# Two attention layers over 16 graphs: TensorE's items dealt anew over the steps, with new places for loads and statistics

## The chip, the cores and the metric

One core of one Trainium2 chip. The metric is the device time of one launch in microseconds. Before the change it is 2078.54 us, the median of 3 runs (2071.99 to 2079.57).

## The reference

For each of 16 graphs `x` is (512, 384) and `adj` (512, 512), all float32, 12 heads of 32:

```
h = relu(layernorm(x)); q, k, v = h@Wq+bq, h@Wk+bk, h@Wv+bv
s = q k^T / sqrt(32) + beta*adj, masked where adj <= 0;  x = x + softmax(s) v          (layer 0)
h = relu(layernorm(x)); q, k, v = h@Wq^T, h@Wk^T, h@Wv^T+bv
s = q k^T / sqrt(384) + 2*adj, rows that are all zero give 0; x = x + softmax(s) v @ Wo^T + bo  (layer 1)
```

## The kernel before, in words

The 32 graph passes (16 graphs in layer 0, then 16 in layer 1; `g`) are cut into 3 chunks `c` of 4 heads, and each chunk into 4 steps `t`, one for each 128 query rows: 12 steps a graph, written below as step 0 to step 11. In a step VectorE (DVE) adds bias and takes the row minimum of four score tiles (`scores`, L340), ScalarE (ACT) takes the exponentials (`exp`, L458), and DVE transposes the tile of the step before in blocks of 32 (`turn`, L353) into `pt`; the tile of t = 3 is instead transposed by TensorE (`tp`, L230) and copied by ACT into `pl`. SyncE moves `pt` to `pk` with 16 DMAs a chunk (`move`, L180), in two halves, and TensorE multiplies P by V in three parts (`pv`, L292): 128 columns from `pl`, twice 192 from `pk`.

Every engine runs its own list in the order written, and waits on counting semaphores. TensorE's (PE's) step holds the scores of the next step, then items that `in_step` (L43) lists: projections `qk` (9 matmuls) and `v` (9), `hT`, `tp`, `post`, and in layer 1 `zero` and `spread`. All results of items go through a ring of three PSUM banks. ACT and DVE copy them out in the next step.

GpSimd (POOL) has the list on which the loads stand (L703 to L747). It issues the loads of `adj` (`load_adj`), of the layer's input into `xin` (`load_x`) and into `res` (`load_residual`), and the store. Between them it does arithmetic that waits for those loads or for other engines: the bias of the next graph in layer 0 (`bias`, four tiles, L595 to L599), the scaling and residual sum of layer 0 (`add_residual`, L633 and L636), adding bv to v (`add_bv`, L606), the row sums of adj in layer 1 (`sum_bias`, L620 to L624), and the scalars of the layernorm (`rstd`, L579 to L585). An add, a wait and an issue that stand later on this list do not start before the earlier ones.

DVE takes the statistics of the next graph's `xin` (`stats`, L398) at steps 0 and 4, the first of them waiting for `load_x`; ACT applies them (`relu`, L465) at steps 5 and 6; `hT` transposes the result at step 7, after which `xin` is free and `load_x` may fetch the graph after it (step 8).

Of the kernel before, what the change touches and what calls it, by code (L numbers as in the profile page):

```python
# [12 lines left out]
HD = D // H  # L13
P = 128
# [9 lines left out]
PARTS = 1 + HALVES  # L24
GRAPHS = 2 * B

# [10 lines left out]

def chunk(s):

    return s // DT, s % DT  # L40


def in_step(g, c, t):  # L43

    g0, a0 = chunk(DT * g + c - 1)
    g1, a1 = chunk(DT * g + c + 1)
    out = []
    if t == 0:
        out += [("zero", g, c)]
    if t == 1:  # L50
        out += [("qk", g1, 2 * a1)]
    if t == 2:
        out += [("qk", g1, 2 * a1 + 1)]
    if t == 3:
        out += [("spread", g0, a0)]
        out += [("tp", g, HC * c + j) for j in range(HC)]
    if layer_of(g) == 0:
        more = {
            (0, 0): [("v", g, 2)],
            (0, 3): [("v", g, 3)],  # L60
            (1, 1): [("post", g - 1, 0), ("post", g - 1, 1)],
            (1, 2): [("post", g - 1, 2), ("post", g - 1, 3)],
            (1, 3): [("hT", g + 1, i) for i in range(DT)],
            (2, 0): [("v", g + 1, 0)],
            (2, 3): [("v", g + 1, 1)],
        }
    else:
        more = {
            (0, 1): [("v", g, 2)],
            (0, 3): [("v", g, 3)],  # L70
            (1, 1): [("post", g - 1, 0), ("post", g - 1, 1)],
            (1, 2): [("post", g - 1, 2)],
            (1, 3): [("hT", g + 1, i) for i in range(DT)],
            (2, 0): [("post", g - 1, 3)],
            (2, 1): [("v", g + 1, 0)],
            (2, 3): [("v", g + 1, 1)],
        }
    return [x for x in out + more.get((c, t), []) if exists(*x)]


def exists(kind, g, i):
    return 0 <= g < GRAPHS and (layer_of(g) == 1 or kind not in ("zero", "spread"))


def step_before(g, c, t):

    n = (DT * g + c) * NT + t - 1
    return in_step(*chunk(n // NT), n % NT) if n >= 0 else []


def pv_in_step(g, c, t):

    if t == TURNS:
        return None
    s = DT * g + c - (2 if t == 0 else 1)
    return (*chunk(s), (2, 0, 1)[t]) if s >= 0 else None


OPENING = [("hT", 0, i) for i in range(DT)] + [("qk", 0, 0), ("qk", 0, 1), ("v", 0, 0), ("v", 0, 1)]
CLOSING = [("spread", GRAPHS - 1, DT - 1)] + [("post", GRAPHS - 1, i) for i in range(NT)]  # L100


def ring_places():

    steps = [x for g in range(GRAPHS) for c in range(STEPS) for t in range(NT) for x in in_step(g, c, t)]
    slot, replaces, held = {}, {}, [None] * RING
    for n, x in enumerate(OPENING + steps + CLOSING):
        slot[x], replaces[x] = n % RING, held[n % RING]
        held[n % RING] = x
    return slot, replaces  # L110
# [7 lines left out]
def two_layers(nc, x, adj, weights, bq, bk, bv, bo, beta, x1, out, mem):  # L118
# [7 lines left out]
    per_graph = {"qk": 2 * DT, "hT": DT, "v": NT, "post": NT, "zero": DT, "spread": DT, "tp": HC * DT}  # L126
    x_in, x_out = (x, x1), (x1, out)
    with ExitStack() as ctx:
# [18 lines left out]
        scaled, res_added, bo_added = sem("scaled"), sem("res_added"), sem("bo_added")  # L147

# [4 lines left out]
        def nth(kind, g, i):  # L153
            return per_graph[kind] * (g - B if kind in ("zero", "spread") else g) + i + 1

        def tokens(dram):
            return dram.rearrange("(t p) n -> p t n", p=P)

# [4 lines left out]
        def _(sp):  # L163
# [6 lines left out]
            def move(g, c):  # L170

                s = DT * g + c
                sp.wait_ge(turned, TURNS * (s + 1))
                for half in range(HALVES):
                    if s:
                        sp.wait_ge(pv_ready, PARTS * (s - 1) + half + 2)
                    for n in range(QUADS):
                        for a in (half, half + HALVES):
                            to = (a - half + n) % QUADS
                            sp.dma_start(m.pk[HD * to:HD * (to + 1), a], m.pt[HD * a:HD * (a + 1), s % 2, to]).then_inc(moved[layer_of(g)][c][half], 16)  # L180

            sp.dma_start(m.xin[:], tokens(x[0])).then_inc(x_first, 16)
            sp.dma_start(m.beta[:], beta.rearrange("(a n) -> a n", a=1).to_broadcast([P, 1])).then_inc(small_in, 16)
            sp.dma_start(m.bq[:], bq).then_inc(small_in, 16)
            sp.dma_start(m.bk[:], bk).then_inc(small_in, 16)
            for n in range(3):
                load_weight(0, n)
            load_row(m.bva, bv[0], bv_in[0])
            load_row(m.bvx, bv[1], bv_in[1])
            for g in range(GRAPHS):  # L190
                for c in range(STEPS):
# [10 lines left out]
                    if (g, c) == (B, 1):  # L202
                        sp.wait_ge(res_added, NT * B)
                        sp.dma_start(m.wo[:], weights[1][3].rearrange("(t p) n -> p t n", p=P)).then_inc(wo_in, 16)

        @block.tensor
        def _(pe):
            halves = [(t, x, y) for t in range(DT) for x, y in ((0, 0), (0, 1), (1, 0))]
# [13 lines left out]
            def item(kind, g, i):  # L222
                to = m.ring[:, slot[kind, g, i], :]
                if replaces[kind, g, i]:
                    pe.wait_ge(done[replaces[kind, g, i][0]], nth(*replaces[kind, g, i]))
                if kind == "tp":
                    s, j = DT * g + i // HC, i % HC
                    pe.wait_ge(exp_done, UNITS * s + HC * TURNS + j + 1)
                    for n in range(QUADS):
                        mm = nc.tensor.transpose(to[:, P * n:P * (n + 1)], m.s[:, TURNS % 2, j, P * n:P * (n + 1)], m.ident[:])  # L230
                if kind == "hT":
# [3 lines left out]
                if kind == "qk":  # L235
                    pe.wait_ge(done["hT"], nth("hT", g, DT - 1))
                    if i < 2 and g % B == 0:
                        pe.wait_ge(weights_split[i], layer_of(g) + 1)
                    w, a = (m.wq, m.wk)[i % 2], i // 2
                    for n, (t, x, y) in enumerate(halves):  # L240
                        mm = nc.tensor.matmul(to, w[y][:, t, P * a:P * (a + 1)], m.hT[x][:, t, :], start=n == 0, stop=n == 3 * DT - 1)  # L241
                if kind == "v":
                    if i == 0:
# [3 lines left out]
                    for n, (t, x, y) in enumerate(halves):  # L247
                        mm = nc.tensor.matmul(to[:, 0:D], m.hT[x][:, t, P * i:P * (i + 1)], m.wv[y][:, t, :], start=n == 0, stop=n == 3 * DT - 1)  # L248
                if kind == "zero":
                    at = (g + i) % 2  # L250
                    pe.wait_ge(ksum_done, nth("zero", g, i))
                    for t in range(NT):
                        mm = nc.tensor.matmul(to[:, HC * t:HC * (t + 1)], m.q[:, at, P * t:P * (t + 1)], m.ksum[:, at, :], start=True, stop=True)
                if kind == "spread":
                    pe.wait_ge(recip_done, nth("spread", g, i))
                    for t in range(NT):
                        mm = nc.tensor.transpose(to[:, P * t:P * (t + 1)], m.rwide[:, t, :], m.ident[:])
                if kind == "post":
# [4 lines left out]
                    for t in range(DT):  # L263
                        o = m.oT[:, t, P * i:P * (i + 1)]
# [4 lines left out]
                mm.then_inc(ready[kind], 1)  # L269

            def pv(g, c, part):
# [3 lines left out]
                if part == 0:  # L275
# [4 lines left out]
                    pe.wait_ge(done["tp"], nth("tp", g, HC * c + HC - 1))  # L280
                else:
                    pe.wait_ge(moved[layer_of(g)][c][part - 1], MOVES * (g % B + 1))
                    quads = slice(part - 1, QUADS, HALVES)
                for n in range(QUADS):
                    for j in range(HC):
                        to = m.out[HD * j:HD * (j + 1), :]
                        if part == 0:
# [546 lines left out]
```

## Time and profile before

| | us |
|---|---|
| profiled execution | 2081.65 |
| its span, first to last instruction | 2079.9 |
| PE busy | 1952.3 (94%) |
| DVE busy | 1834.6 (88%) |
| ACT busy | 1660.9 (80%) |
| POOL busy | 912.6 (44%) |
| DMA engines, queue of SyncE / of GpSimd | 60.0% / 19.0% |

Busy time counts an engine as busy while an instruction runs; waits don't count. The shares hide that the two layers differ: one graph of layer 0 and one of layer 1 have to be read apart.

### The profile page before, as it was taken

Reading aid. Unit: us, or ns where it says so; the run is one execution under the profiler, and the core shown is the slowest. Engines: PE = TensorE matmul, PEld = TensorE weight load, DVE = VectorE, ACT = ScalarE, POOL = GpSimd, SP = SyncE. Lnnn points to the kernel's source line nnn. Section 1 sums busy time; section 2 is a strip of 40 time slices with the busy share of each in tenths; the row PEclk is TensorE's granted clock in tenths of the full one; section 3 lists DMA queues with packets and bytes.
Section 4 is the critical chain, followed back from the end, with each engine's and each line's share of the span. In section 5 each row is a group of like instructions: output and inputs, shape, how many; then the busy total and the mean of one; then the engine's idle time right before and its main releaser. Section 6 shows DMA issues by size and latency. Waiting matters only on the chain.

```text
span 2079.9 us, 49656 instructions
## 1 busy us (share of the span) xinstructions
PE 1952.3 (94%) x18240; PEld 1256.6 (60%) x18240; DVE 1834.6 (88%) x3992; ACT 1660.9 (80%) x4215; POOL 912.6 (44%) x1115
## 2 busy tenths in 40 slices
PE   5999999999999999998999999999999999999995
PEld 3666566666656666555666666666666666666663
DVE  5999999999999999997988988898889988898873
ACT  4898888989889998888877777787777777777771
POOL 6365655555555655533434332442334332342321
PEclk9999999999999999998999999999999999999997
DMA  3888978988788988887878778787788778787675
GB/s 128 199 206 220 239 205 219 236 227 222 206 215 220 236 218 220 230 215 198 210 199 221 179 185 201 185 212 185 178 202 217 183 185 203 179 218 185 161 182 134
DMA packets 105105, 419.04 MB, mean 201 GB/s; under 512 B 27216, under 2 KB 30800, under 8 KB 104864
## 3 DMA queue, kind: packets, MB, share of 16 engines
q1 hardware_dynamic: 77920, 307.60, 60.0%
q0 software_dynamic: 26944, 108.27, 19.0%
q8 instruction: 146, 2.39, 0.5%
q14 instruction: 95, 0.78, 0.1%
HBM read 88.61 MB, written 25.17 MB: 55 GB/s over the span
## 4 chain that ended last, share of the span: by engine, by line
PE 43%; DVE 13%; ACT 12%; DMA 10%; issue 9%; POOL 9%; SPq 4%; DVEq 0%; POOLq 0%; ACTq 0%
PE ring L241 11%; PE sc L219 9%; PE out L292 8%; ACT s L458 7%; DVE s L340 7%; PE ring L266 7%; DMA bias<-in_adj 5%; DVE pt L353 5%; DMA pk<-pt 4%; PE ring L248 4%; SPq L180 4%; ACT pl L480 3%; POOL mask L595 2%; PE ring L230 2%; POOL bias L599 2%
## 5 line engine op out<-in xcount | busy, mean ns | idle before, releaser
L458 ACT ACTIVATE s<-s,nmax 128x512 f32<-128x512 f32 x1536 | 1095.2, 728 | 271.7 <-DVE nmax L340 271.3
L340 DVE CUSTOM_DVE_ANT_0 s<-sc,bias 128x512 f32<-128x512 f32 x1536 | 968.5, 687 | 75.8 <-PE sc L219 55.4
L353 DVE STREAM_TRANSPOSE pt<-s 128x2048 f32<-128x2048 f32 x288 | 664.0, 2306 | 0.3 <-issue 0.3
L219 PE MATMUL sc<-k,q 32*128 32x512 f32 x3072 | 444.8, 648 | 54.8 <-DVE nmax L340 46.2
L292 PE MATMUL out<-pk,v 128*32 128x192 f32 x6144 | 297.2, 335 | 30.4 <-DMA pk<-pt 30.4
L458 ACT ACTIVATION_READ_ACCUMULATOR s<-s,nmax 128x1 f32 x1536 | 314.6, 205 | 0.0
L292 PEld LDWEIGHTS out<-pk,v 128*32 128x32 f32 x6144 | 182.7, 111 | 180.1 <-issue 95.8
L248 PE MATMUL ring<-wv,hT 128*128 128x384 f32 x1152 | 236.5, 350 | 0.0
L241 PE MATMUL ring<-hT,wq 128*128 128x512 f32 x864 | 230.4, 411 | 1.5 <-DVE hT L366 1.5
L241 PE MATMUL ring<-hT,wk 128*128 128x512 f32 x864 | 227.5, 407 | 0.9 <-ACT q L490 0.9
L219 PEld LDWEIGHTS sc<-k,q 32*128 32x128 f32 x3072 | 122.8, 185 | 166.5 <-DVE nmax L340 91.7
L241 PEld LDWEIGHTS ring<-hT,wq 128*128 128x128 f32 x864 | 157.2, 191 | 107.5 <-issue 74.0
L241 PEld LDWEIGHTS ring<-hT,wk 128*128 128x128 f32 x864 | 155.3, 188 | 104.1 <-issue 65.2
L230 PE MATMUL ring<-ident,s 128*128 128x128 f32 x1536 | 200.9, 280 | 11.0 <-ACT pl L480 6.6
L248 PEld LDWEIGHTS ring<-wv,hT 128*128 128x128 f32 x1152 | 196.0, 189 | 21.3 <-issue 16.8
L230 PEld LDWEIGHTS ring<-ident,s 128*128 128x128 f32 x1536 | 166.9, 142 | 64.9 <-issue 45.7
L480 ACT ACTIVATE pl<-ring 128x512 f32<-128x512 f32 x384 | 198.1, 606 | 8.3 <-PE ring L230 8.3
L606 POOL TENSOR_TENSOR v<-v,bvx 128x384 f32<-128x384 f32 x64 | 65.2, 1018 | 315.7 <-ACT v L506 315.7
L606 POOL TENSOR_TENSOR v<-v,bva 128x384 f32<-128x384 f32 x64 | 64.8, 1013 | 272.9 <-ACT v L506 272.9
L595 POOL TENSOR_SCALAR mask<-bias 128x512 f32<-128x512 f32 x64 | 124.3, 1942 | 108.5 <-DMA bias<-in_adj 107.0
L266 PE MATMUL ring<-wo,oT 128*128 128x384 f32 x384 | 139.3, 508 | 1.0 <-DVE oT L389 1.0
L340 DVE DVE_READ_ACCUMULATOR2_ANT nmax<- 128x1 f32 x1536 | 127.7, 83 | 0.0
(82 smaller groups left out, 1889.3 us busy)
## 6 DMA issues: line engine op xcount, KB each, us to landing
pk<-pt SPq DMA_DIRECT2D x1536, 192.0 KB, 5.4
bias<-in_adj POOLq DMA_DIRECT2D x32, 1024.0 KB, 11.8
res<-in_x POOLq DMA_DIRECT2D x16, 768.0 KB, 14.7
x_between<-res POOLq DMA_DIRECT2D x16, 768.0 KB, 8.6
xin<-x_between POOLq DMA_DIRECT2D x16, 768.0 KB, 9.9
res<-x_between POOLq DMA_DIRECT2D x16, 768.0 KB, 10.1
out_x<-res POOLq DMA_DIRECT2D x16, 768.0 KB, 7.6
xin<-in_x POOLq DMA_DIRECT2D x15, 768.0 KB, 7.9
```

Source lines behind the costliest of these rows:

```text
L219: mm = nc.tensor.matmul(m.sc[:, j, :], m.q[rows, s % 2, P * t:P * (t + 1)], m.k[rows, s % 2, :], start=True, stop=True)
L230: mm = nc.tensor.transpose(to[:, P * n:P * (n + 1)], m.s[:, TURNS % 2, j, P * n:P * (n + 1)], m.ident[:])
L241: mm = nc.tensor.matmul(to, w[y][:, t, P * a:P * (a + 1)], m.hT[x][:, t, :], start=n == 0, stop=n == 3 * DT - 1)
L248: mm = nc.tensor.matmul(to[:, 0:D], m.hT[x][:, t, P * i:P * (i + 1)], m.wv[y][:, t, :], start=n == 0, stop=n == 3 * DT - 1)
L266: mm = nc.tensor.matmul(to[:, 0:D], o, m.wo[:, t, :], start=t == 0, stop=t == DT - 1)
L292: mm = nc.tensor.matmul(to, v[:, n, P * c + HD * j:P * c + HD * (j + 1)], p, start=n == 0, stop=n == QUADS - 1)
L340: nc.vector.tensor_tensor_reduce(out=m.s[:, t % 2, j, :], in0=m.sc[:, j, :], in1=m.bias[g % 2][:, t, :], scale=s_scale[layer], scalar=3.0e ...
L353: nc.vector.transpose(out=to, in_=m.s[:, t % 2].rearrange("p j (i a e) -> p (j i) a e", a=QUADS, e=HD)).then_inc(turned, 1)
L458: nc.scalar.activation(tile, tile, ACT.Exp, bias=m.nmax[s % 2][:, t, j:j + 1], scale=-1.0, accum_out=m.sums[s % 2][:, t, j:j + 1]).then_in ...
L480: nc.scalar.activation(m.pl[:, j, :], frm, ACT.Copy).then_inc(done["tp"], 1)
L595: nc.gpsimd.tensor_scalar(m.mask[:], tile, 0.0, masked, ALU.is_le, ALU.mult).then_inc(mask_done, 1)
L606: nc.gpsimd.tensor_tensor(v, v, (m.bva, m.bvx)[layer_of(g)][:], ALU.add).then_inc(v_added, 1)
```

## The change

- The rules of `in_step` give way to a table `PLACES` with a place, in steps, for every item. `qk` and `v` are done in two pieces of 5 and 4 matmuls (`qk_first`, `qk`), between which other items may stand.
- P times V is two parts of 256 columns. `pt` and `pk` hold five row tiles each instead of `pt` double and `pl`; even and odd chunks share the middle one, so that `turn` of t = 2 now also waits for the moves of the chunk just before.
- `zero` in layer 1 (4 matmuls of 4 columns with 128 columns of weights) becomes `sums` (4 of 128 columns with 32 columns of weights), a copy by ACT, and one transpose (`zero`).
- The last chunk is turned by PE and copied by ACT, without moves; the last `post` accumulates in the score banks, and each row tile is stored by its own DMA. At the start x and two weights are loaded first, and adj after x.
- Statistics are all at step 0, `relu` at step 2, `load_x` at step 10, `load_adj` at step 2 (layer 0) or 6 (layer 1), `load_residual` at 6 or 2, the bias tiles at steps 3, 4, 5 and 7; `add_bv`, `add_residual` and the store follow their item's place.

```diff
+PLACES = ({
+    "qk_first": (-3.54, -2.95, -1.21, 0.29, 4.48, 5.62),
...
+OUT_STEP = ((9, 9, 8), (10, 10, 10))
+STATS_STEP, RELU_STEP = (-12, -12), (-10, -10)
+X_STEP, ADJ_STEP, RES_STEP, BIAS_STEPS = 10, (2, 6), (6, 2), (3, 4, 5, 7)
...
 def turn(g, c, t):
-                if t == 0 and s >= 2:
-                    g2, a2 = chunk(s - 2)
+                last = {0: s - 2, TURNS - 1: s - 1}.get(t, -1)
+                if last >= 0:
+                    g2, a2 = chunk(last)
                     for half in range(HALVES):
                         dve.wait_ge(moved[layer_of(g2)][a2][half], MOVES * (g2 % B + 1))
...
 # DVE, in a step
-                if g + 1 < GRAPHS:
-                    if (c, t) == (0, 0):
-                        stats(g + 1, (0, 1))
-                    if (c, t) == (1, 0):
-                        stats(g + 1, (2, 3))
-                        aggregate(g + 1)
+                for half, at in enumerate(STATS_STEP):
+                    ahead = graph_at(g, c, t, at)
+                    if ahead:
+                        stats(ahead, (2 * half, 2 * half + 1))
+                        if half:
+                            aggregate(ahead)
...
 # POOL, in a step
+                for x in step_before(g, c, t):
+                    if x[0] == "v":
+                        add_bv(*x[1:])
                 if g + 1 < GRAPHS:
+                    if at == ADJ_STEP[layer]:
...
                         load_adj(g + 1)
...
                     if layer_of(g + 1) and (c, t) == (2, 2):
                         sum_bias(g + 1)
-                    if g + 2 < GRAPHS and (c, t) == (2, 0):
+                    if at == X_STEP and g + 2 < GRAPHS:
                         pool.wait_ge(ready["hT"], nth("hT", g + 1, DT - 1))
                         load_x(g + 2)
+                ahead = graph_at(g, c, t, STATS_STEP[1])
+                if ahead:
+                    rstd(ahead)
                 if g:
-                    if g > 1 and (c, t) == (0, 1):
+                    if g > 1 and at == RES_STEP[layer_of(g - 1)]:
                         load_residual(g - 1)
...
+                if g + 1 < GRAPHS and layer_of(g + 1) == 0 and at in BIAS_STEPS:
+                    bias(g + 1, BIAS_STEPS.index(at))
```

POOL in layer 0, before, from the store of one graph's result on (`mask`, `bias`: the bias tiles; `wo`, `res`: `add_residual`, whose scratch is `wo`):

```order
L572 DMA x_between<-res 128x4x384
L606 TENSOR_TENSOR v<-v,bva 128x384
L559 DMA bias<-in_adj 128x4x512
L606 TENSOR_TENSOR v<-v,bva 128x384
L565 DMA res<-in_x 128x4x384
L595 TENSOR_SCALAR mask<-bias 128x512
```

The load of `res` stands ahead of the first arithmetic on the new `bias`. After, from the `adj` load on:

```order
L671 DMA bias<-in_adj 128x4x512
L718 TENSOR_TENSOR v<-v,bva 128x384 x2
L707 TENSOR_SCALAR mask<-bias 128x512
...
L711 TENSOR_TENSOR bias<-bias,mask 128x512
L677 DMA res<-in_x 128x4x384
L745 TENSOR_TENSOR wo<-wo,recip 128x384
...
L748 TENSOR_TENSOR res<-res,wo 128x384
L718 TENSOR_TENSOR v<-v,bva 128x384
L668 DMA xin<-in_x 128x4x384
```

Now three bias tiles stand between the two loads, and two tiles of `add_residual`, the fourth bias tile, a third `add_residual` and `v` between `res` and `xin`.

POOL in layer 1, before, around the load of `xin` (`room` from L671 is `keep`'s result, from L620 to L624 the row sums):

```order
L556 DMA xin<-x_between 128x4x384
L659 TENSOR_SCALAR mz<-nmax 128x16
...
L671 TENSOR_TENSOR room<-recip,mz 128x512
L606 TENSOR_TENSOR v<-v,bvx 128x384
L620 TENSOR_TENSOR room<-bias 128x512
...
L624 TENSOR_TENSOR room<-room 128x128
```

And after:

```order
L783 TENSOR_TENSOR room<-recip,mz 128x512
L718 TENSOR_TENSOR v<-v,bvx 128x384
L732 TENSOR_TENSOR room<-bias 128x512
...
L736 TENSOR_TENSOR room<-room 128x128
L668 DMA xin<-x_between 128x4x384
```

The load has moved from ahead of `keep`, `v` and the row sums to behind all three.

## Rows read from the trace of the kernel before

**Rows 1.** Three stretches: length, busy us of PE, PEld, DVE, ACT, POOL, clock, DMA, GB/s
```profile
57.55:931.42 873.87, 828.61 (x8146) 529.46 (x8146) 820.31 (x1786) 782.58 (x1974) 479.07 (x467) 0.99 0.86 219
1066.37:1933.68 867.31, 850.54 (x7722) 551.32 (x7722) 771.90 (x1693) 661.09 (x1704) 312.74 (x481) 1.00 0.78 194
463.00:520.79 57.79, 54.83 (x546) 35.08 (x538) 54.70 (x120) 52.27 (x133) 32.80 (x33) 1.00 0.87 224
```

**Rows 2.** Waits in 463.00 to 520.79: us in total, times, longest
```profile
DVE hT L366 <- ACT hT L483: 1.5, 1, 1.5
DVE s L340 <- PE sc L219: 1.0, 2, 0.6
```

**Rows 3.** Timeline of PE, layer 1: start us, us, what
```profile
1444.16 1.51 PE L292 MATMUL out<-pk,v 128*32 128x192 f32 x32
1445.60 1.06 PE L253 MATMUL ring<-ksum,q 128*128 128x4 f32 x8
...
1448.07 2.37 PE L241 MATMUL ring<-hT,wq 128*128 128x512 f32 x9
1450.37 1.08 PE L292 MATMUL out<-pl,v 128*32 128x128 f32 x32
1451.38 1.85 PE L248 MATMUL ring<-wv,hT 128*128 128x384 f32 x9
...
1459.52 1.99 PE L230 MATMUL ring<-ident,s 128*128 128x128 f32 x16
```

**Rows 4.** Timeline of POOL, one graph of layer 0
```profile
473.45 0.84 POOL L633 TENSOR_TENSOR wo<-wo,recip 128x384 f32<-128x384 f32 x1
...
477.21 1.92 POOL L595 TENSOR_SCALAR mask<-bias 128x512 f32<-128x512 f32 x1
...
481.54 0.83 POOL L556 DMA_DIRECT2D xin<-in_x  x1
...
501.92 0.77 POOL L559 DMA_DIRECT2D bias<-in_adj  x1
...
514.53 1.92 POOL L595 TENSOR_SCALAR mask<-bias 128x512 f32<-128x512 f32 x1 [8.46 <-DMA bias<-in_adj]
```

**Rows 5.** Timeline of DVE, layer 0: two turns, one step apart
```profile
503.17 2.31 DVE L353 STREAM_TRANSPOSE pt<-s 128x2048 f32<-128x2048 f32 x1
...
508.05 2.31 DVE L353 STREAM_TRANSPOSE pt<-s 128x2048 f32<-128x2048 f32 x1
```

**Rows 6.** The load of adj, L559, in 60 to 900
```profile
DMA to landing us min/median/max: 9.3/11.7/12.6
```

**Rows 7.** The load of x, L556, in 60 to 900
```profile
DMA to landing us min/median/max: 5.3/8.0/12.8
```

**Rows 8.** The load of the residual, L565, in 60 to 900
```profile
DMA to landing us min/median/max: 13.5/14.8/15.4
```

**Rows 9.** The load of x, L556, in 1100 to 2000
```profile
DMA to landing us min/median/max: 8.3/9.8/13.0
```

**Rows 10.** Timeline of POOL, layer 1, steps 10 and 11
```profile
1500.38 1.02 POOL L606 TENSOR_TENSOR v<-v,bvx 128x384 f32<-128x384 f32 x1 [9.57 <-ACT v L506]
1501.35 1.31 POOL L620 TENSOR_TENSOR room<-bias 128x512 f32<-128x512 f32 x1
...
1507.03 0.82 POOL L572 DMA_DIRECT2D out_x<-res  x1 [0.30 <-POOL room L624]
```

**Rows 11.** Timeline of DVE, layer 1, step 0 of the next graph
```profile
1509.54 0.95 DVE L398 BATCH_NORM_STATS2 stats<-xin 128x6 f32<-128x384 f32 x2
```

**Rows 12.** Timeline of PE, layer 0: the matmuls behind a long wait
```profile
521.69 2.79 PE L292 MATMUL out<-pk,v 128*32 128x192 f32 x32 [2.68 <-DMA pk<-pt]
```

**Rows 13.** Chain of waits at the end: start us, us, what
```profile
2041.24 2.23 DVE pt L353
...
2053.79 5.66 DMA pk<-pt
2059.50 2.83 PE out L292 x32
```

**Rows 14.** Timeline of DVE at the start
```profile
10.19 1.93 DVE L398 BATCH_NORM_STATS2 stats<-xin 128x6 f32<-128x384 f32 x4
```

More of the change, by code:

```diff
@@ L1 @@
+import math
 from contextlib import ExitStack
@@ L23 @@
 HALVES = 2
-PARTS = 1 + HALVES
+PARTS = HALVES
 GRAPHS = 2 * B
@@ L35, in layer_of, with turned_place, order_of @@
     return g // B
+LAST = GRAPHS * DT - 1
+LAST_PLACES = (3, 4, 2, 1)
+def turned_place(s, t):
+    return t if s % 2 == 0 else NT - t
+def order_of(s, t):
+    if s == LAST:
+        return LAST_PLACES[t] - 1
+    return (t + 1) % NT if s % 2 == 0 else t if t == TURNS else TURNS - 1 - t
 def chunk(s):
     return s // DT, s % DT
-def in_step(g, c, t):
[L45 to L78, printed above, removed]
@@ L125, in two_layers @@
     m = mem
-    per_graph = {"qk": 2 * DT, "hT": DT, "v": NT, "post": NT, "zero": DT, "spread": DT, "tp": HC * DT}
+    per_graph = {"qk": 2 * DT, "hT": DT, "v": NT, "post": NT, "sums": DT, "zero": DT, "spread": DT, "tp": HC * DT, "turn": 0}
     x_in, x_out = (x, x1), (x1, out)
@@ L153, in nth, with leaving, graph_at @@
         def nth(kind, g, i):
-            return per_graph[kind] * (g - B if kind in ("zero", "spread") else g) + i + 1
+            return per_graph[kind] * (g - B if kind in ("sums", "zero", "spread") else g) + i + 1
         def tokens(dram):
             return dram.rearrange("(t p) n -> p t n", p=P)
+        def leaving(g, c, t):
+            back = [(chunk(s), number(g, c, t) - NT * s) for s in range(max(DT * g + c - 3, 0), DT * g + c + 1)]
+            return [out for out, n in back if n == OUT_STEP[layer_of(out[0])][out[1]]]
+        def graph_at(g, c, t, at):
+            n = number(g, c, t) - at
+            return n // (NT * DT) if n % (NT * DT) == 0 and 0 < n // (NT * DT) < GRAPHS else None
         def steps():
@@ L473, in item @@
             def item(kind, g, i):
+                if kind == "pv" or kind in FIRST or (kind, layer_of(g)) == ("post", 1):
+                    return
                 frm = m.ring[:, slot[kind, g, i], :]
+                if kind == "turn":
+                    t, j = i // HC, i % HC
+                    act.wait_ge(ready["turn"], i + 1)
+                    if j == 0 and t != 1:
+                        for half in range(HALVES):
+                            act.wait_ge(moved[1][DT - 3 if t == 0 else DT - 2][half], MOVES * B)
+                    nc.scalar.activation(m.pt[:, :, LAST_PLACES[t], j].rearrange("p a (i e) -> p i a e", e=HD),
+                                         frm.rearrange("p (i a e) -> p i a e", a=QUADS, e=HD), ACT.Copy).then_inc(done["turn"], 1)
                 if kind == "tp":
@@ L733, in _ @@
                         load_residual(g - 1)
[L734 removed]
+                    if layer_of(g - 1) and (c, t) == (1, 0):
                         add_bo(g - 1)
[L736 to L740 removed]
@@ L741, in _ @@
-                if g + 1 < GRAPHS and layer_of(g + 1) == 0 and (c, t) == (1, 3):
-                    bias(g + 1, TURNS)
+                for old in range(max(g - 2, 0), g):
+                    if layer_of(old) == 0:
+                        for i in range(NT):
+                            if number(g, c, t) == step_of("post", old, i) + 2:
+                                add_residual(old, i)
+                    if number(g, c, t) == step_of("post", old, NT - 1) + 2:
+                        store(old)
```

306 lines of the change are left out of this document (189 added, 117 removed).

## The prediction

> **What bounds the kernel now.** I read the busy time by stretch first, because the two layers have different limits. The stretches are cut where POOL starts `rstd`, once a graph. Fifteen graphs of layer 0 take 873.87 us, 58.26 each, and thirteen of layer 1 take 867.31, 66.72 each [rows 1]. In layer 1 PE is busy 850.54 us of them, 98%: PE is the limit. In one undisturbed graph of layer 0 (57.79 us) PE has 54.83 and DVE 54.70, and neither fills it; the waits say that DVE stood still 1.5 us for `hT` from ACT and 1.0 for scores from PE [rows 1, 2]. Without these, DVE's own list would take about 57.8 - 2.5 = 55.3 us. So before looking at anything else there are at most 3 us a graph to win in layer 0, and in layer 1 what PE's list loses. POOL is busy 55% and 36% of the stretches, and nobody would call it a limit. But it is one list with three loads on it, and the question that the change raises is how long once around that list takes, waits for the loads included.
>
> **PE's own work.** In layer 1 PE stands without gaps, so the distance between two starts is the price of an item [rows 3]. A part of 192 columns costs 1.44 us (1444.16 to 1445.60), one of 128 costs 1.01 (1450.37 to 1451.38). 64 columns more cost 0.43, so 256 cost 1.87. Per chunk 1.01 + 2 x 1.44 = 3.89 becomes 2 x 1.87 = 3.74: 0.15 less, 0.45 a graph. `zero` takes 1.06 and at least 0.9 of PE; its four matmuls of 4 columns cannot be cheaper than their weight loads. The new `sums` is a quarter of a 128-column part, 0.25 to 0.3, and one transpose a sixteenth of 1.99, 0.13 [rows 3]. That saves 0.5 a chunk, 1.5 a graph of layer 1. Cutting 9 matmuls into 5 and 4 costs nothing that I can see: 2.30 us for nine (1448.07 to 1450.37) is 0.26 each, and no weights are loaded twice. I take 0, with 0.1 a cut as the other end. PE's list in layer 1 so falls by 2 us from 65.4 to about 63.4, in layer 0 by 0.45. If nothing else came late, layer 1 would take 64.4 us a graph.
>
> **POOL's loop in layer 1.** DVE takes all statistics of the next graph at step 0, and nothing behind them on DVE starts until `xin` has landed; PE then waits for DVE's scores. `xin` is now issued at step 10, behind `add_bv` of v(0) and behind the row sums. v(0) is made by PE at the end of step 9. How long is it from the statistics to that `add_bv`? Before, the statistics start at 1509.54 [rows 11] and the add at 1500.38 of the graph before [rows 10], so at 1567.1 one period later: 57.5 us. DVE now has four tiles and `aggregate` at this point instead of two, 1.4 us more. PE's list between the two (steps 1 to 9) loses 1.31 us in parts of PV (3 x 1.01 + 4 x 1.44 = 8.79 against 4 x 1.87 = 7.48), 1.27 in a projection of which five matmuls moved into step 0, 0.94 in `zero`, and gains a `spread` of 0.5: 3.0 less. So 57.5 + 1.4 - 3.0 = 55.9. Then the add 0.97, the row sums 5.68 (1501.35 to 1507.03) [rows 10], and the load 9.8 (8.3 to 13.0) [rows 9]: 72.4 us until the next statistics can start. This is a closed loop, and it is longer than PE's 64.4. PE then stands still for some 8 us a graph. Behind a wait of 2.68 us a 192-column part took 2.79 us instead of 1.51, 1.3 more [rows 12], which is the lower of PE's two clock levels for a while. I add 0.6 for it (half of it falls under DVE's next scores), with 0 and 2.6 as ends. The period is 73.0 us, 6.3 more than now; the ends are 70.9 and 78. It holds for graphs 17 to 30, 14 x 6.3 = +88. Graph 15 (row sums already stand ahead of its load) and graph 16 (short `post`) get 5 each by estimate, +10. The last graph has no load behind it: -3.
>
> **POOL's loop in layer 0.** From the start of the statistics: 1.9 + 0.4 for them (0.95 per two tiles [rows 11]), scores of step 1 2.5, one step of 4.9 [rows 5], and ACT copies v(1) 0.5 later; `add_bv` 1.0. That is 11.2, and only then does POOL issue `adj`. It lands 11.7 later [rows 6], at 22.9; in rows 4 the first bias tile does stand still for this load, from 501.92 to 514.53. Three bias tiles at 4.33 (477.21 to 481.54) [rows 4] end at 35.9. Only now `res` is issued, since it was moved behind them. Its landing is not shown without the `adj` load issued just ahead of it: with it 14.8 [rows 8], while x of the same size takes 8.0 [rows 7]. I take 9, near x, for `adj` has landed by then but the moves of chunk 1 run; 44.9. Then `add_residual` 0 and 1 (3.76, 473.45 to 477.21), bias tile 3 (4.33), `add_residual` 2 (1.88) and v(0) (0.97): 55.8. Then x, 8.0: 63.8 us until the next statistics. Against 58.26 that is +5.5 a graph. The lower end takes 9.3, 5.3 and 5.3 for the loads: 55.0, and then DVE's 55.3 decides. The upper takes 12.6, 15.4 and 12.8: 75.9. The loop is whole for graphs 2 to 14; graphs 0 and 1 lack the `res` part. 13 x 5.5 = +72.
>
> By the Trainium skill, DMA: Bandwidth & Descriptors, section Anatomy of one DMA, a load from this queue would take about 2.0 us plus its bytes over 436 KB a microsecond: 3.8 us for x or `res`, 4.4 for `adj`. The rows show two to three times that. With those figures the layer 0 loop would be 63.8 - 7.3 - 5.2 - 4.2 = 47 us, and the layer 1 loop 66.4, and the loads would be all but hidden.
>
> **What this cover hides.** In layer 0 the first part of PV of chunk 0 moves to about 9 us after the third turn, and the eight moves of a half take 8 issues of 0.64 us (16 in 10.3) and 5.66 to land [rows 13], 10.8, so PE would stand for about 2 us; `turn` of t = 2 may find half 1 of the chunk before still moving, 0 to 5 us. Both lie inside the 8 us in which DVE would wait for x anyway: I cost them at 0. If x came in time they would cost 1 to 4 us a graph. The extra ACT copy of `sums` costs nothing: ACT is busy 76% in layer 1. ACT's copy of `post` 3 waits for `add_residual` 0, which ends at 46.8 in the loop; ACT stands some 5 us there, before DVE would stand for x, so it is in the same time. The balanced steps of PE (3.9 to 7.1 us in layer 1 by these prices, 2.5 to 8.5 before) win nothing while DVE waits for x.
>
> **Opening and closing.** At the end the last turn ends at 2043.47, then 16 issues and 5.66 us of landing stand ahead of the last part of PV at 2059.50 [rows 13]. With transposes and ACT copies (four after the last exponential) the two parts can start at about 2045.5 and the last at 2047.5: 12 us earlier. The output projection no longer waits for the last scaling (1 us), and a store of 192 KB lands earlier than one of 768 KB (3). Together -16, between -8 and -20. At the start the statistics begin when x has landed, at 10.19 [rows 14], beside the adj load and three weights; with x alone in front -3, between 0 and -4.
>
> **Sum**, against the profiled execution of 2081.65: +72 + 88 + 10 - 3 - 16 - 3 = +148, 2230; that execution is 3 us above the median of the runs, so **2227 us**.
>
> **Rivals.** *Loads hidden, faster.* If loads land in about 4 us, or POOL reaches them earlier than I think, layer 0 falls to about 56 and layer 1 to 66.4: 2078.5 - 15 x 2.3 - 14 x 0.3 - 19 = 2021. For it speaks PE's shorter list; against it that no x load of layer 1 landed in under 8.3 us [rows 9]. It turns when the three landings of layer 0 sum to under 23 us instead of the 28.7 that I use (58.26 less the 35.1 of the rest of the loop), and when x in layer 1 lands in under 4. *Only layer 1.* The layer 0 loop is made of three landings that I know only in another order; if `res` lands in 6 and `adj` in 9.5, DVE's list decides at about 57: 2078.5 - 15 x 1.3 + 88 + 10 - 3 - 19 = 2135. *Late loads.* If loads and moves collide as `adj` and `res` do now, layer 0 takes 70 and layer 1 76 us: +152 + 130 + 10 - 22, 2349. That PE's table does not take effect is excluded by the order of its items.
>
> **Chances.** 0.62 for the forecast (its own range 2150 to 2310), 0.14 for layer 1 alone, 0.13 for the faster case, 0.11 for late loads. The range 2115 to 2320 takes in the second case and leaves the last two out, about 2 in 10. A change of 0.5% is about what a measurement of this kernel can tell; faster by more 0.13, within 0.03 (a mixture of small gains and losses), slower 0.84.
>
> **What the changed profile would show.** Right: DVE's statistics with an idle time of 5 to 10 us before them, released by the load of `xin`, once a graph in both layers; `xin` issued right behind the row sums in layer 1; POOL's first `add_residual` waiting for `res`; a graph of layer 1 at 73, of layer 0 at 64; PE busy below 90% in both; parts of 256 columns 1.87 us apart. Wrong: no wait ahead of the statistics, PE at 98% in layer 1, and a graph of 64 us there. If the waits of DVE name the moves instead, the two costs that I put at nothing are the real ones. A period of 58 or less in layer 0 with landings of 5 us would mean the second case.

## The result, and the profile after

The changed kernel takes 2125.73 us (median; 2119.51 to 2135.22), the kernel before beside it 2079.06 (2071.99 to 2081.4): ratio 1.0234, 95% interval 1.0183 to 1.0285. It is slower, as forecast, but by 47 us and not by 148. The profiled execution took 2130.47 us, 48.8 more than that of before.

I cut the span at POOL's `rstd` again, once a graph. It now stands in step 0 and not in step 4, so the cuts lie earlier than in [rows 1], but the stretches hold the same 15 and 13 graphs. Columns as there:

```profile
41.47:911.83 870.36, 810.66 (x6646) 498.42 (x6642) 818.33 (x1778) 779.67 (x1965) 483.51 (x470) 0.99 0.85 218
1048.67:1969.56 920.89, 841.93 (x6522) 510.96 (x6525) 775.18 (x1691) 681.55 (x1742) 311.92 (x482) 0.97 0.69 184
```

Layer 0: 870.36 / 15 = 58.02 us a graph (before 58.26). Layer 1: 920.89 / 13 = 70.84 (before 66.72), and 13 x 4.12 = 53.6. So -3.5 in layer 0, +53.6 in layer 1, and all that lies outside the two stretches (opening, transition, closing) together -1.3, where the forecast's terms come to -12: the 48.8. PE in layer 1 was busy 98% and is now 91%: it stands still, at a mean granted clock of 0.97.

What it stands for, in layer 1 (who waited for whom, us in total, times, longest; unlike rows 2 this is the stretch of 13 graphs):

```profile
PE sc L275 <- DVE nmax L422: 78.2, 46, 5.2
DVE pt L436 <- issue: 75.3, 34, 4.9
DVE res L466 <- PE ring L341: 20.6, 26, 1.6
DVE stats L483 <- DMA xin<-x_between: 6.4, 12, 1.3
```

PE waits for DVE, and DVE waits mostly in `turn` (L436): 75.3 / 13 = 5.8 us a graph. For `stats`, where I had put the whole loss, it is 0.5. "issue" means that this view names no event that released the turn. The chain of waits does say what came last. Over one such turn (start us, us, what):

```profile
1429.26 1.91 PE out L368 x32
1431.18 0.51 SPq L228
...
1435.22 0.60 SPq L228
...
1435.86 4.12 DMA pk<-pt
1439.98 1.36 issue
1441.34 2.32 DVE pt L436
```

A part of PV ends, which frees its half of `pk`'s shared tile; SyncE issues the eight moves of this half, the last of them 4.7 us after the first. The chain's row of 4.12 us is not its landing: the row is cut where DVE's earlier work ends (1439.98), and the rest stands as "issue". How long these eight moves took from issue to landing is shown by themselves:

```profile
DMA to landing us min/median/max: 4.0/4.9/5.4
```

The last one lands 5.4 us after its issue at 1435.86, and 0.1 us later the third turn starts, 12.1 us after PE began that part. The pattern comes again at 1419.18 (last landing 6.3 us after its issue) and 1466.52.

In layer 0 no `stats` wait shows, and the turn waits for nothing that matters:

```profile
PE out L368 <- DMA pk<-pt: 33.1, 29, 2.8
PE sc L275 <- DVE nmax L422: 26.0, 66, 2.3
DVE s L422 <- PE ring L292: 24.8, 15, 1.7
```

The last row is new: DVE waits 1.65 us once a graph for the fourth transpose (`tp`) of chunk 0, which the table sets at place 4.02, just inside step 4.

The landings, which carried both loops of my forecast, in the order x in layer 0, x in layer 1, `adj` in layer 0, `res` in layer 0 (answering to [rows 7], [rows 9], [rows 6] and [rows 8]):

```profile
DMA to landing us min/median/max: 4.7/4.8/4.9
DMA to landing us min/median/max: 5.1/5.4/6.1
DMA to landing us min/median/max: 5.6/5.9/7.9
DMA to landing us min/median/max: 4.7/4.8/5.3
```

The same loads took 8.0, 9.8, 11.7 and 14.8 us before.

### The profile page after: what moved, and what is told of

Its sections match the earlier page's. It is cut to its first block, busy times and chain, and to the rows that moved or that the text cites. A ratio compares the mean times of both kernels' runs of the same rounds, so it can differ in the third digit from the quotient of the medians.

```text
span 2128.7 us, 43980 instructions
## 1 busy us (share of the span) xinstructions
PE 1921.5 (90%) x15264; PEld 1173.7 (55%) x15264; DVE 1831.9 (86%) x3989; ACT 1690.4 (79%) x4275; POOL 912.5 (43%) x1114
## 4 chain that ended last, share of the span: by engine, by line
PE 29%; SPq 23%; DVE 21%; DMA 14%; issue 7%; ACT 1%; POOL 1%; DVEq 0%; POOLq 0%; ACTq 0%
SPq L228 23%; DMA pk<-pt 13%; DVE s L422 12%; DVE pt L436 8%; PE out L368 7%; PE sc L275 7%; PE ring L310 6%; PE ring L292 3%; PE ring L341 3%; PE ring L318 1%; ACT s L546 1%; DMA res<-in_x 1%; DMA room<-in_wq 0%; PE ring L301 0%; PE ring L331 0%
## 5 line engine op out<-in xcount | busy, mean ns | idle before, releaser
L436 DVE STREAM_TRANSPOSE pt<-s 128x2048 f32<-128x2048 f32 x285 | 657.4, 2307 | 85.9 <-issue 85.0
L368 PE MATMUL out<-pk,v 128*32 128x256 f32 x6080 | 376.6, 389 | 38.0 <-DMA pk<-pt 37.9
L546 ACT ACTIVATION_READ_ACCUMULATOR s<-s,nmax 128x1 f32 x1536 | 305.5, 199 | 0.0
L579 ACT ACTIVATE pk<-ring 128x512 f32<-128x512 f32 x380 | 206.7, 599 | 103.5 <-PE ring L292 103.5
L310 PE MATMUL ring<-hT,wq 128*128 128x512 f32 x864 | 256.0, 431 | 2.6 <-DVE hT L451 2.6
L318 PE MATMUL ring<-wv,hT 128*128 128x384 f32 x1152 | 246.8, 350 | 0.0
L310 PE MATMUL ring<-hT,wk 128*128 128x512 f32 x864 | 239.5, 409 | 0.0
L292 PEld LDWEIGHTS ring<-ident,s 128*128 128x128 f32 x1536 | 172.9, 143 | 95.5 <-issue 41.4
L292 PE MATMUL ring<-ident,s 128*128 128x128 f32 x1536 | 213.6, 283 | 1.5 <-ACT s L546 1.5
L310 PEld LDWEIGHTS ring<-hT,wq 128*128 128x128 f32 x864 | 162.3, 200 | 70.3 <-issue 29.3
L341 PE MATMUL ring<-wo,oT 128*128 128x384 f32 x360 | 125.3, 491 | 0.0
```

The costliest lines, as they stand in the source:

```text
L341: mm = nc.tensor.matmul(to[:, 0:D], o, m.wo[:, t, :], start=t == 0, stop=t == DT - 1)
L368: mm = nc.tensor.matmul(to, v[:, n, P * c + HD * j:P * c + HD * (j + 1)], p, start=n == 0, stop=n == QUADS - 1)
L436: nc.vector.transpose(out=to, in_=m.s[:, t % 2].rearrange("p j (i a e) -> p (j i) a e", a=QUADS, e=HD)).then_inc(turned, 1)
L546: nc.scalar.activation(tile, tile, ACT.Exp, bias=m.nmax[s % 2][:, t, j:j + 1], scale=-1.0, accum_out=m.sums[s % 2][:, t, j:j + 1]).then_in ...
L579: nc.scalar.activation(to.rearrange("p a (i e) -> p i a e", e=HD), frm.rearrange("p (i a e) -> p i a e", a=QUADS, e=HD), ACT.Copy).then_in ...
```

## The experiments

Each kernel was timed with the kernel before on the same chip. Theory M (moves; the expectations call it theory A): the shared tile of `pt` and `pk` ties the third turn to the moves of the chunk before, and these to parts of PV. Theory X (theory B there): the late load of x is the limit, as forecast. L0 and L1 are the us a graph of the profiled run, over the same 15 and 13 graphs.

| kernel | us | ratio [95%] | L0 | L1 |
|---|---|---|---|---|
| after | 2125.73 | 1.0234 [1.0183, 1.0285] | 58.02 | 70.84 |
| e1 PV parts earlier in layer 1 | 2101.97 | 1.0100 [1.0063, 1.0136] | 58.02 | 69.31 |
| e2 x at step 8, both layers | 2155.61 | 1.0354 [1.0303, 1.0404] | 60.02 | 70.30 |
| e3 before + the third turn's wait | 2289.96 | 1.0997 [1.0949, 1.1045] | 66.75 | 71.77 |
| e4 e1 + layer 0's `tp`, `pv` | 2102.54 | 1.0101 [1.0065, 1.0137] | 58.08 | 69.37 |
| e5 e1 + x at step 8 in layer 1 | 2077.38 | 0.9982 [0.9959, 1.0005] | 58.04 | 67.38 |
| e6 e5 + statistics split | 2074.37 | 0.9957 [0.9937, 0.9978] | 57.96 | 67.14 |
| e7 e5 + `zero` as before | 2077.58 | 0.9981 [0.9962, 1.0000] | 58.01 | 67.60 |
| e8 e5 + projections whole | 2120.43 | 1.0192 [1.0145, 1.0239] | 58.94 | 70.45 |
| e9 e6 + one `post` later | 2081.44 | 0.9996 [0.9974, 1.0017] | 57.96 | 67.43 |
| e10 after, no shared tile | 2067.31 | 0.9940 [0.9920, 0.9961] | 57.83 | 66.97 |
| e11 e10 + x at step 8 in layer 1 | 2014.75 | 0.9688 [0.9656, 0.9721] | 57.97 | 63.18 |
| e12 before, `res` moved | 2070.61 | 0.9964 [0.9948, 0.9981] | 57.94 | 66.83 |
| e13 after, x at step 8 in layer 1 | 2122.85 | 1.0216 [1.0168, 1.0263] | 58.03 | 69.80 |
| e14 e11 + `zero` as before | 2037.72 | 0.9816 [0.9779, 0.9854] | 57.84 | 64.49 |
| e15 e11 + projections whole | 2055.18 | 0.9898 [0.9855, 0.9940] | 58.99 | 64.60 |

### The first three: is it the moves or x?

e1:

```diff
-    "pv": (7.95, 9.19, 11.45, 12.58, 14.74, 17.36),
+    "pv": (7.95, 8.75, 11.45, 11.90, 14.74, 16.30),
```

> The changed kernel with the second part of PV in layer 1 placed earlier (chunk 0 at 8.75 instead of 9.19, chunk 1 at 11.90 instead of 12.58, chunk 2 at 16.30 instead of 17.36), nothing else. Theory A (the third turn of a chunk waits for the moves of the chunk before, because both use the middle place of pt, and the moves of half 1 are released only by the second part of PV): the idle time before the turns, 75.3 us in 13 graphs of layer 1, nearly goes, a graph of layer 1 falls from 70.8 to 65 to 67 us, the total from 2126 to 2035 to 2070. Theory B (POOL's list with the three loads sets the period, my prediction): nothing on that list changes, so 2126 within 10, and the wait moves to the statistics.

e2:

```diff
-X_STEP, ADJ_STEP, RES_STEP, BIAS_STEPS = 10, (2, 6), (6, 2), (3, 4, 5, 7)
+X_STEP, ADJ_STEP, RES_STEP, BIAS_STEPS = 8, (2, 6), (6, 2), (3, 4, 5, 7)
```

> The changed kernel with the load of x issued at step 8 again, ahead of bv and the row sums; nothing else. Theory A: the statistics waited for x only 6.4 us in 13 graphs, so the total stays at 2126 within 10, or rises a little if x now meets the moves: its landing goes from 5 us back to 8 to 10. Theory B: each graph of layer 1 loses its wait for x, 4 us or more, so the total falls by 50 us or more.

e3, in `turn` of the kernel before, where `pt` and `pk` are not shared and the wait is not needed:

```diff
+                if t == TURNS - 1 and s >= 1:
+                    g2, a2 = chunk(s - 1)
+                    for half in range(HALVES):
+                        dve.wait_ge(moved[layer_of(g2)][a2][half], MOVES * (g2 % B + 1))
```

> The kernel before, with one wait added: the third turn of a chunk also waits for the moves of the chunk just before, as in the changed kernel, though the buffer is its own. Theory A in its weak form (the wait costs only because the parts of PV that release the moves stand late): before, half 1 is released at step 8 of its chunk instead of 8.6 to 9.4, so there is 3 to 5 us more room; the time stays at 2079 to 2095. Theory A in its strong form (any such wait costs): 2110 to 2130. Theory B: 2079, no change.

e1's waits in layer 1, and what the load of x did there:

```profile
DVE res L466 <- PE ring L341: 34.0, 13, 2.6
DVE stats L483 <- DMA xin<-x_between: 29.4, 13, 3.0
DVE s L422 <- PE sc L275: 26.6, 30, 2.9
DVE pt L436 <- issue: 23.6, 22, 3.2
```

Three parts of PV set 0.44 to 1.06 steps earlier take 24 us off, and the turn's wait from 75.3 to 23.6. So the moves are a cause. But the time fits neither expectation (2102, not 2035 to 2070 and not 2126): 23.0 us come back as a wait for x (6.4 to 29.4). Theory X is right too, one layer below.

e2 shows that x alone is not the cause; it is 30 us slower, where theory M had at most "a little". In layer 1 its `stats` no longer wait, the turn still waits 71.0, and the graph takes 70.3. In layer 0 it makes things worse, and that is the first row on what a landing costs. The load of x of layer 0, e2:

```profile
DMA to landing us min/median/max: 7.8/10.6/12.0
```

And the waits of e2 in layer 0:

```profile
PE sc L275 <- DVE nmax L422: 54.4, 76, 2.8
DVE pt L436 <- issue: 32.5, 17, 3.0
```

Two steps earlier the same load takes 10.6 us and not 4.8, with moves in flight beside it; and the third turn, which waited 1 us or less in e1, waits up to 3.0 for moves that share the engines with the load.

e3 missed both expectations: the wait alone costs the old kernel 210 us, the most in layer 0 (66.75 us a graph, waits of up to 7.9). Its layer 0 waits:

```profile
PE sc L219 <- DVE nmax L340: 131.3, 52, 7.9
DVE pt L357 <- issue: 118.9, 30, 7.9
```

In the old kernel the moves of a chunk end too late for it. The old order of PV and the new wait don't go together, and the new table had been dealt for the wait: what the wait costs in the new kernel can't be read from e3. (PE's granted clock in its layer 0 is 0.94, against 0.99 before.) It does show that a wait on the chunk before, added to an order that isn't made for it, is no small term.

### Tuning what the first three had shown

e4 adds to e1, in layer 0:

```diff
-    "tp": (3.02, 3.33, 3.74, 4.02, 7.17, ...
+    "tp": (3.02, 3.33, 3.74, 3.95, 7.17, ...
-    "pv": (5.35, 6.99, ...
+    "pv": (5.80, 6.99, ...
```

> As the kernel with the earlier second parts in layer 1, and in layer 0 the fourth transpose of chunk 0 at step 3 (3.95 instead of 4.02) and the first part of PV of chunk 0 behind the five matmuls of the projection (5.80 instead of 5.35). Theory A with waits of layer 0 read from the trace (DVE waits 1.65 us a graph for that transpose, PE 2.2 us for the moves): a graph of layer 0 gets 0.5 to 1 us shorter, 8 to 15 us in all below the run with layer 1 alone. Theory B: no change, since POOL's list is the same.

The wait for `tp` (24.8 us) is gone, but DVE's wait for scores of PE rises to 31.5, from 14.4 in e1. Nothing is won where 8 to 15 us were expected: layer 0's 58 us is DVE's list with PE's close behind, and a wait taken away there comes up in the next step.

e5 sets x at step 8 in layer 1 and leaves layer 0 at 10:

```diff
-X_STEP, ADJ_STEP, RES_STEP, BIAS_STEPS = 10, (2, 6), (6, 2), (3, 4, 5, 7)
+X_STEP, ADJ_STEP, RES_STEP, BIAS_STEPS = (10, 8), (2, 6), (6, 2), (3, 4, 5, 7)
```

> The kernel with the earlier second parts of PV in layer 1 (2102 us), and there the load of x at step 8, ahead of bv and the row sums (layer 0 keeps step 10). Theory A+ (with the turns' wait shortened, POOL's loop is the next limit of layer 1: its statistics wait 29.4 us in 13 graphs for x): that wait goes, a graph of layer 1 falls from 69.3 by 1 to 2 us to 67.5 to 68.3, the total to 2075 to 2090. Rival (the wait for x only fills time in which DVE would wait for the moves or PE anyway): 2102 within 8.

With both causes weakened, layer 1 falls to 67.38, as expected, and the kernel is as fast as before. e6 splits the statistics of layer 1 over two steps:

```diff
-STATS_STEP, RELU_STEP = (-12, -12), (-10, -10)
+STATS_STEP, RELU_STEP = ((-12, -12), (-12, -8)), ((-10, -10), (-7, -6))
```

> As the one with x at step 8, and in layer 1 the statistics at steps 0 and 4 and relu at steps 5 and 6, as in the kernel before. If DVE's longer step 0 (four tiles and the aggregate, 2.3 us) is what leaves PE waiting for scores in step 1, a graph of layer 1 gets 0.5 to 1 us shorter, 7 to 15 us in all; if not, no change within 8 us.

e6 is 3 us below e5, which is the expectation's "no change": DVE's longer step 0 costs next to nothing. Of the variants of the new table that compute everything it is the fastest, 0.9957 [0.9937, 0.9978]. e7 goes back from `sums` and a transpose to the four small matmuls of `zero`, at e5's other settings:

```diff
-    "sums": (0.40, 5.95, 9.55),
-    "zero": (3.77, 6.57, 10.02),
+    "zero": (0.40, 5.95, 9.55),
```

> As the one with x at step 8, but with the old row sums of the scores in layer 1: four matmuls of 4 columns against 128 columns of weights at the places of sums, no copy by ACT and no transpose. The prediction had the new form 0.5 us a chunk cheaper on PE, 24 us over 48 chunks. If PE still sets the pace of layer 1, the total is 15 to 25 us above the run with x at step 8; if DVE's waits set it, within 8.

No difference from e5: behind DVE's waits the form of `zero` does not show. e8 does the projections in one piece, each where its second piece stood:

```diff
-    "qk_first": (-3.19, -1.51, 0.47, 2.05, 4.48, 5.78),
+    "qk_first": (-3.081, -1.391, 1.459, 2.689, 4.739, 5.829),
...
-    "v_first": (-2.23, -1.30, 1.29, 2.25),
+    "v_first": (-2.091, -0.851, 1.499, 3.119),
```

> As the one with x at step 8, but with each projection in one piece, at the place of its second piece. Matmuls, weights and results are the same. If cutting costs PE something at each place where another item stands between the pieces, this is 5 to 20 us faster; if the pieces help by filling PE's steps evenly, it is 5 to 20 us slower; the prediction had 0.

43 us slower than e5, more than twice what either expectation allowed. e9 moves one item of e6 and is 7 us slower, a miss:

```diff
-    "post": (18.16, 18.40, 20.89, 21.19),
+    "post": (18.16, 18.40, 21.05, 21.19),
```

> As the one with earlier second parts of PV, x at step 8 and split statistics (2074 us), with the third output projection of a graph in step 9 (21.05 instead of 20.89). DVE waited 44 us in 13 graphs for these projections, 2.6 us of each graph at the third, because step 8 holds 8.2 us of PE's work and step 9 only 5.2. If that is the next limit, 5 to 20 us faster, 2055 to 2070; if not, within 5.

### Each cause alone

Because e5 still has both waits in part, e10 gives every chunk its own place, and e13 moves only x. e10's `pt` has six tiles; what it leaves out to make room stands in its expectation, and e11, e14 and e15 leave out the same, so that these four do not compute the layer in full; number and size of the instructions stay.

```diff
-                self.pt = sb("pt", [P, QUADS, NT + 1, HC, P])
+                self.pt = sb("pt", [P, QUADS, 2 * TURNS, HC, P])
...
-                last = {0: s - 2, TURNS - 1: s - 1}.get(t, -1)
+                last = {0: s - 2}.get(t, -1)
```

> The changed kernel with six row tiles in pt, so that no two chunks share one and the third turn waits for no moves; the places of all items are unchanged. The room comes from what is left out: the low half of hT lies on the high half (the projections lose their second term) and layer 1 adds bo instead of bv to v; number and size of all instructions are the same but one load of 192 KB. Theory A: the turns' wait (75.3 us in 13 graphs of layer 1) is gone, the wait of the statistics for x appears in its place (20 to 40 us, as with the earlier parts of PV), the last chunk loses its 9 us wait for moves: 2080 to 2105. Theory A without a second limit: 2030 to 2060. If the shared tile is not the cause: 2126 within 10.

e11 is e10 with x at step 8 in layer 1, as in e5:

> As the one with six row tiles (same parts left out), and the load of x at step 8 in layer 1. Both limits named so far are then gone: 2050 to 2075, a graph of layer 1 at 65 to 67 us; with only one of them real, no better than the run with six tiles.

e13 is the changed kernel with that line of e5 alone:

> The changed kernel with nothing but the load of x at step 8 in layer 1 (layer 0 keeps step 10). It fills the fourth corner of the square: changed 2126, six tiles 2067, six tiles and x at step 8 2015, and this. If the two waits of layer 1 lie side by side and the shared tile's is the later one, removing the other alone gives nothing: 2126 within 10. If they add up, it gives the same 52 us as behind the six tiles: 2074.

The waits of DVE in layer 1, e10:

```profile
DVE stats L482 <- DMA xin<-x_between: 42.5, 13, 3.8
DVE res L465 <- PE ring L340: 16.3, 26, 0.6
```

of e13:

```profile
DVE pt L436 <- issue: 68.2, 31, 3.4
DVE res L466 <- PE ring L341: 21.5, 26, 1.8
```

and the stretch of layer 1 in e11, columns as above:

```profile
1046.38:1867.74 821.36, 816.24 (x6514) 497.23 (x6513) 769.89 (x1691) 674.31 (x1743) 312.39 (x481) 1.00 0.79 206
```

Four kernels make a square, in us a graph of layer 1:

| | x at step 10 | x at step 8 |
|---|---|---|
| shared tile | 70.84 (after) | 69.80 (e13) |
| own tiles | 66.97 (e10) | 63.18 (e11) |

e10's 2067 us lies between its two expectations, e11's 2015 is 35 us below its own, e13 came as expected for waits side by side. Without either wait PE is busy 816.24 of 821.36 us, 99.4%. With the late x alone the loop takes 3.8 us more than PE, with the shared tile alone 6.6, with both 7.7 and not 10.4: the waits lie beside each other and the longer decides. That is why x at step 8 gives 3 us alone (the intervals overlap) and 53 without the shared tile.

### The two terms of PE, measured where PE is the limit

e14 is e11 with e7's edit, e15 is e11 with e8's.

> As the one with six tiles and x at step 8 (2015 us, layer 1 at 63.2 us a graph with PE busy 99%; the same parts left out), with the old form of zero. Behind the shared tile the two forms took the same time. If PE is the limit now, the prediction's term shows: 0.5 us a chunk, 1.5 a graph of layer 1, 24 us in all, so 2030 to 2042. If not, 2015 within 6.

> As the one with six tiles and x at step 8 (same parts left out), with each projection in one piece. Behind the shared tile that cost 43 us. If the pieces only kept PE's steps from delaying the parts of PV and with them the moves, the cost nearly goes without the shared tile: 2015 to 2030. If they fill PE's waits for their own sake, it stays: 2040 to 2065.

The same stretch of e14 and of e15:

```profile
1044.31:1882.66 838.35, 832.28 (x6474) 521.67 (x6474) 773.36 (x1691) 669.64 (x1704) 312.85 (x482) 1.00 0.78 202
```

```profile
1062.84:1902.59 839.75, 811.80 (x6521) 498.74 (x6520) 770.22 (x1690) 673.85 (x1743) 312.30 (x481) 1.00 0.77 201
```

The old `zero` costs 23 us, which e7 could not show behind DVE's waits. It is work: PE is busy 16 us longer in this stretch, 1.2 a graph. The whole projections cost 40 us in another way, 18.4 in the stretch of layer 1 and 15.2 in that of layer 0. In layer 1 PE is busy 4.4 us less than in e11, but stands still 28 us of the stretch and not 5. What it stands for, in e15:

```profile
PE sc L274 <- ACT k L600: 16.1, 26, 0.8
PE sc L274 <- DVE nmax L421: 8.9, 13, 0.7
```

e11 has 2.4 us of the second and none of the first. So the pieces earn their 40 us by when the results of a step come, not by PE's work. The edit did two things at once, though: it joined the pieces, and it did the first five matmuls at the place of the last four, up to 1.5 steps later. Which of the two costs the 40 us is not shown; whole projections were tried at no other place.

### A load by itself

e12 is the kernel before with one issue moved, `res` of layer 0 from right behind the `adj` load (step 1) to behind the first bias tile (step 3):

```diff
-                    if g > 1 and (c, t) == (0, 1):
+                    if g > 1 and (c, t) == ((0, 1) if layer_of(g - 1) else (0, 3)):
```

> The kernel before, with the load of the residual in layer 0 moved from step 1 to behind the first bias tile of step 3, when adj has landed. It tests the landing times on which my loop in layer 0 stood. If a landing depends on what else is in flight, the residual lands in 5 to 8 us instead of 14.8, and adj (alone then) in 7 to 10 instead of 11.7; if the chip needs that long for 768 KB anyhow, 12 or more. Total within 10 of 2081, since nothing waits for it.

The landing of `res` in e12, where [rows 8] had 14.8:

```profile
DMA to landing us min/median/max: 8.5/9.8/10.8
```

So `res` lands 5.0 us sooner without the `adj` load just ahead of it, which lies between the two expectations. `adj` missed its own: it takes 12.1 us without `res` behind it, no less than the 11.7 before. Its landing in e12, and then what SyncE's queue, the moves, carried while one such `adj` load was in flight, in the kernel before, in e12 and in the changed one (packets, MB, share):

```profile
DMA to landing us min/median/max: 9.1/12.1/13.3
```

```profile
q1 hardware_dynamic: 383, 1.56, 55.0%
q1 hardware_dynamic: 462, 1.89, 69.3%
q1 hardware_dynamic: 158, 0.59, 43.9%
```

In these three windows `adj` lands fast (5.9 us) where few moves stand beside it. The kernel gains 0.4% (interval 0.9948 to 0.9981), of an issue that was moved and nothing else.

## Why the prediction was right in direction and wrong in size

**The direction came by luck.** The forecast's own mechanism, the late x, is the only one of the two waits left in e10, and e10 is not slower than the kernel before (0.9940). The kernel is slower because of a wait that I had put at nothing. The first step that failed is the sum of the three landings in layer 0, the second the third turn at 0.

**PE's own work: right.** A part of PV of 256 columns was forecast at 1.87 us; in PE's timeline the distance to the next start is 1.86 (the 1.93 beside it is the length of the part, whose end is modelled):

```profile
1416.74 1.93 PE L368 MATMUL out<-pk,v 128*32 128x256 f32 x32
1418.60 1.14 PE L275 MATMUL sc<-k,q 32*128 32x512 f32 x8
```

PE's list in layer 1 was forecast at 63.4 us and a graph that nothing else delays at 64.4; in e11 PE is busy 62.8 us a graph and the graph takes 63.18. `zero` was put at 1.5 us a graph, 24 us in all; e14 measured 1.3 and 23.

**Projections in pieces, "I take 0": wrong.** The number is right for PE's busy time and wrong for the kernel: whole projections at the places of their second pieces cost 40 us (e15) and 43 (e8). I had counted an item's price and not the place it takes. I wrote that the balanced steps "win nothing while DVE waits for x"; DVE waits for x far less than that.

**POOL's loop in layer 0, +5.5 a graph: wrong, and this was the largest miss.** Measured -0.24. The step that failed is the sum of three landings, 11.7 + 9 + 8.0 = 28.7. They are 5.9 + 4.8 + 4.8 = 15.5. With 35.1 for the rest the loop is 50.6 us, under DVE's list of 55.3, and hidden. In the forecast's own words it turns at 23. The trace has this slack: before it issues x POOL waits 4.13 us for v, and x, issued at 492.59, lands 2.3 us before the statistics start:

```profile
491.64 1.01 POOL L718 TENSOR_TENSOR v<-v,bva 128x384 f32<-128x384 f32 x1 [4.13 <-ACT v L611]
```

```profile
499.70 1.88 DVE L483 BATCH_NORM_STATS2 stats<-xin 128x6 f32<-128x384 f32 x4
```

The order of POOL was as I said, but I had taken the durations from an order in which these loads ran together and beside the moves, and put them in one that no longer has that company. The 16 DMA engines while x is in flight, before (8.0 us) and after (4.8 us); the last two numbers are their busy share and GB/s:

```profile
481.60:489.60 8.00, 7.75 (x94) 5.19 (x90) 7.96 (x20) 8.00 (x23) 6.23 (x8) 1.00 0.98 246
```

```profile
492.60:497.40 4.80, 4.45 (x33) 2.50 (x26) 4.67 (x10) 3.49 (x11) 3.46 (x5) 1.00 0.54 165
```

For x the engines are full before and half free after. Their share alone doesn't tell the landing: while `adj` is in flight after (510.50 to 516.40) they are 97% busy at 278 GB/s, 1.03 of the 1.64 MB for `adj` itself, and it lands in 5.9 us. The Trainium skill's rule that I had weighed and put aside (DMA: Bandwidth & Descriptors, Anatomy of one DMA) gives 3.8 and 4.4 us, against 4.8 and 5.9 measured here: 20 to 25% short. The rows of before (8.0 and 11.7) were 67 to 98% too long. (The forecast's "two to three times that" holds for x and `adj`; the 14.8 of `res` is 3.9 times.)

**POOL's loop in layer 1, 73.0: half right.** With a landing of 5.4 and not 9.8, the forecast's own sum is 55.9 + 0.97 + 5.68 + 5.4 = 68.0. e10, in which this loop is the only one left, takes 66.97. So the mechanism is there and costs 3.8 us a graph against PE's 63.2, but in the changed kernel another wait hides it.

**The third turn, "I cost them at 0": wrong, and it is the cause of the slowdown.** With tiles of its own (e10) the kernel is 58 us faster; with x early instead (e13) only 3. I had weighed it for layer 0 alone, where it costs little, put it in the shadow of the wait for x, and left layer 1 out. There the parts of PV stand late (places 9.19, 12.58, 17.36), and part (1.9), eight issues (4.7) and the last landing (5.4) make 12.1 us, two steps of 5.9. What waits for the part at 9.19 can so start at about 9.19 + 12.1 / 5.9 = 11.2, and the third turn of chunk 2 stands at the beginning of step 11 (in the trace it waits 2.64 us there, at 1466.52). I had the pieces: I used 0.64 us an issue and 5.66 to land at the end of the kernel [rows 13], and did not lay them beside the places of layer 1. The forecast did say what it would mean if the waits of DVE named the moves: that the two costs put at nothing are the real ones. The chain of waits names them.

**Closing, -16: -2.3.** From the end of DVE's last scores to the end of the span is 38.7 us before (from 2041.2), 36.4 after (from 2092.3), and 27.2 in e11. The last chunk has no moves, but ACT writes its turned tiles into the shared `pt`, so it waits for those of the chunk before. Chain of waits of after:

```profile
2086.56 1.91 PE out L368 x32
...
2091.68 1.46 SPq L228
...
2095.28 4.06 DMA pk<-pt
...
2099.44 0.61 ACT pt L571
```

It is the same path, 12.9 us here. Without it the closing gives 11.5 of the 16.

**Opening, -3: 0.** The statistics start at 10.30 and not at 10.19 [rows 14]. x lands by 5.87, when POOL goes on to its `adj` issue, but DVE's list begins with small operands that come last:

```profile
10.16 0.15 DVE L500 TENSOR_SCALAR nbeta<-beta 128x1 f32<-128x1 f32 x1 [10.16 <-DMA bk<-in_bk]
```

I had read the start of the statistics as the landing of x; the row ahead of it said otherwise.

So the nearest case was the rival "only layer 1" (2135), with its number but not its reason, and the number by luck: layer 0's loop is hidden as it says, but layer 1 loses 4.1 us a graph and not 6.3, mostly to the turn and not to x, and the closing gives 2.3 and not 16.

Left open: what of e3's 210 us is the wait and what the clock, why e9's one item costs 7 us, and whether it is the cut or the place of the projections that earns the 40 us. A version with own tiles and everything computed was not tried.

## What to carry to other kernels

A landing belongs to the load and its company: take it from a row in which the same transfers run beside it, or bound it from below by the quietest one. When a buffer is shared, follow the release from the last reader back through every queue (here part of PV, eight issues, landing: 12 us) and lay it beside the place of the writer, in each layer by itself; never cost it at nothing because another wait is expected to cover it. And where two waits of the same engine lie side by side, taking one away shows little: make the square of four kernels.

## What the runs showed of the hardware

A 768 KB load of x lands in 4.8 us with the DMA engines half free and in 10.6 with moves in flight (e2, where only its issue stands two steps earlier); `res` takes 14.8 behind an `adj` load, 9.8 without it (e12), and 4.8 after. It works the other way too: of the moves that e2 issued from 553.8 on, the last, issued at 559.52 beside the load, landed 9.2 us after its issue, against 5.4 in the result's chain, and a third turn waited for it:

```profile
DMA to landing us min/median/max: 4.1/5.1/9.2
```

```profile
559.52 5.95 DMA pk<-pt
...
568.82 2.32 DVE pt L436
```

(The 5.95 is again cut where DVE's earlier work begins.) Only the moves that meet the load are late: over layer 0 the median landing of all moves is 4.2 us in e2 and 4.4 in the changed kernel.
